# Weighted rows scattered by addition into one result per token, instead of two results weighed in the combine

## The reference, cut to what matters

```python
logits = jnp.einsum('bsd,de->bse', x, router_w) + router_b
probs = jax.nn.softmax(logits, axis=-1)
topk_p, topk_i = jax.lax.top_k(probs, 2)
topk_p = topk_p / jnp.sum(topk_p, axis=-1, keepdims=True)
combine = jnp.sum(one_hot(topk_i, 8) * topk_p[..., None], axis=-2)
moe = jnp.zeros_like(x)
for e in range(8):
    moe = moe + combine[..., e:e + 1] * (gelu((x @ w1[e] + b1[e]) * gate[e]) @ w2[e] + b2[e])
shared = (gelu((x @ sw1 + sb1) * sgate) @ sw2 + sb2) * sigmoid(shared_weight)
y = layernorm(moe + shared) * ln_g + ln_b
out = x_attn + tanh(g_ffn) * y        # x = layernorm(x_attn) above
```

## Time and profile before

| | |
|---|---|
| median of 3 runs | 1027.6 us (1027.29 to 1041.74) |
| the profiled execution | 1027.21 us, of which span 1025.4 |
| PE busy | 721.9 us (70%) |
| DVE busy | 741.0 us (72%) |
| POOL busy | 601.7 us (59%) |
| ACT busy | 554.5 us (54%) |
| attention, until about | 512 us (and its last quads until 537) |
| shared expert, until about | 606 us |
| experts' loop, until about | 918 us |
| combine, until | 1025.4 us |

### The profile page before, as it was taken

The page is one execution under the profiler, slowest core; times in us unless marked ns, Lnnn a source line. Parts: engine busy times, 40 slices in busy tenths (PEclk is TensorE's granted clock), DMA queues, the critical chain, the costliest instruction groups (busy, mean ns, idle before and its releaser), DMA issues. The chain is left out here.

```text
span 1025.4 us, 26459 instructions
## 1 busy us (share of the span) xinstructions
PE 721.9 (70%) x7850; PEld 570.9 (56%) x7851; DVE 741.0 (72%) x2078; ACT 554.5 (54%) x1131; POOL 601.7 (59%) x658
## 2 busy tenths in 40 slices
PE   2888778788777788777535899998888888850000
PEld 1556555555555555555424788888888888740000
DVE  5699999988999999889653975444444444436997
ACT  2777656677666677655212345555555554526553
POOL 5454666756666757665518904666666666650544
PEclk9899999999999999998856899999999999985555
DMA  4211222122212123000107201222222222215442
GB/s 119 50 38 47 59 54 61 35 66 62 63 50 59 34 67 84 28 15 30 42 31 228 65 3 52 62 61 60 62 62 62 59 62 57 62 53 153 127 119 82
DMA packets 91301, 66.19 MB, mean 65 GB/s; under 512 B 17009, under 2 KB 80753, under 8 KB 91249
## 3 DMA queue, kind: packets, MB, share of 16 engines
q1 hardware_dynamic: 70048, 35.49, 13.8%
q0 software_dynamic: 8448, 17.45, 5.4%
q10 hardware_dynamic: 12752, 12.58, 3.6%
HBM read 38.21 MB, written 23.09 MB: 60 GB/s over the span
## 5 line engine op out<-in xcount | busy, mean ns | idle before, releaser
L834 POOL TENSOR_TENSOR prob<-prob,mx 128x1024 f32<-128x1024 f32 x64 | 121.6, 1900 | 148.5 <-DVE mx L536 148.4
L1286 POOL DMA_INDIRECT expert_results<-y,dest x136 | 148.7, 1093 | 82.7 <-POOL dest L1282 56.2
L1100 ACT ACTIVATE hT<-bank,b1g_c,gate_c 128x256 f32<-128x256 f32 x272 | 138.1, 558 | 88.2 <-issue 38.5
L166 POOL DMA_INDIRECT expert_lists<-xn,slots x128 | 125.0, 977 | 66.9 <-issue 30.6
L1041 PE MATMUL bank<-w,hT 128*128 x1088 | 139.6, 281 | 24.1 <-ACT hT L1100 20.2
L1041 PEld LDWEIGHTS bank<-w,hT 128*128 128x128 f32 x1088 | 127.2, 191 | 39.2 <-issue 39.2
L366 PE MATMUL bank<-kbd,qg 128*64 128x256 f32 x1024 | 136.6, 407 | 4.6 <-DVE prob L529 2.0
L762 ACT ACTIVATE PT<-bank 128x512 f32<-128x512 f32 x128 | 70.1, 592 | 81.4 <-PE bank L377 80.4
L383 PE MATMUL bank<-w_att,aT 128*128 128x128 f32 x128 | 33.5, 347 | 94.0 <-issue 62.5
L529 DVE TENSOR_TENSOR prob<-bank,mask 128x512 f32<-128x512 f32 x128 | 86.0, 673 | 18.6 <-PE bank L366 14.0
L366 PEld LDWEIGHTS bank<-kbd,qg 128*64 128x64 f32 x1024 | 71.0, 145 | 45.3 <-issue 16.3
(11 more groups left out here) (182 smaller groups left out, 1743.3 us busy)
## 6 DMA issues: line engine op xcount, KB each, us to landing
rows<-expert_lists SPq DMA_DIRECT2D x70, 130.0 KB
yin<-expert_results SPq DMA_DIRECT2D x16, 512.0 KB, 5.3
x_all<-in_x SPq DMA_DIRECT2D x16, 256.0 KB
ctx_in<-in_ctx SPq DMA_DIRECT2D x16, 256.0 KB
pad_k<-in_mask_BxS_ik SPq DMA_DIRECT2D x16, 256.0 KB
xn2T<-x2T ACTq DMA_DIRECT2D x16, 256.0 KB
out<-res ACTq DMA_DIRECT2D x7, 512.0 KB, 3.2
expert_results<-y,dest POOLq DMA_INDIRECT x136
```

What stands on the lines that cost most here:

```text
L166: po.indirect_dma_start(lists[:, :], bass.IndirectOffsetOnAxis(ap=m.slots[:, par, t, k:k + 1], axis=0), m.xn2[:, par, t, :], None).then_in ...
L834: po.tensor_tensor(ps, ps, mx[:, u, :].unsqueeze(2).broadcast_to([P, H, S]), ALU.subtract).then_inc(subbed, 1)
L1100: ac.activation(hT[:, par, c, :], h_ps[par][c // 2][:, (c % 2) * SL:(c % 2 + 1) * SL], ACT.Gelu, bias=b1g_c[:, c, bass.ds(e, 1)], scale=ga ...
L1286: po.indirect_dma_start(results[:, :], bass.IndirectOffsetOnAxis(ap=dest[:, par, h, :], axis=0), y[:, par, h, :], None).then_inc(sent[par] ...
```

## The change

The weights travel with the rows. `ROW` grows from 130 to 132 values: behind first expert and token number stand w1 - w2 and w2. POOL's placing becomes share = (first expert == e) * (w1 - w2) + w2, the weight of this expert for this token, and the destination is the token number itself. DVE multiplies y by share into a new buffer `yw`, and the scatters *add* yw to one row for each token. So the table must be cleared: SP's queue stores zeros, 256 KB a quad in attention and five more at the start of the experts' program, and POOL waits for all of them ahead of the loop. As a token's two experts may stand in steps that follow each other, POOL waits before the scatters of step t until those of step t-1 have landed. In the combine one load a group takes the place of two, one add that of three operations, and ACT's weighing is gone; the 14 steps of the normalisation now all stand among the statistics, and ACT scales one group behind instead of two.

```diff
-ROW = D + 2
+ROW = D + 4
-RB_STEPS = 5
+RB_STEPS = 6
...
+            def clear(q):
+                sp.dma_start(results[bass.ds(q * QW, QW), :].rearrange("(t p) d -> p t d", p=P),
+                             m.zeros[:, :].unsqueeze(1).broadcast_to([P, QT, D])).then_inc(m.zeroed, 16)
             load(0, 0)
             load(1, 1)
+            sp.wait_ge(m.zeros_set, 1)
+            clear(0)
+            clear(1)
             if NQ // 2 > 1:
                 with sp.Fori(1, NQ // 2) as j:
                     load(j * 2, 0)
+                    clear(j * 2)
                     load(j * 2 + 1, 1)
+                    clear(j * 2 + 1)
...
                 elif i == 5:
                     need(ve, rb_step, q, per=RB_STEPS, k=2, total=NQ)
-                    ve.tensor_copy(weight[:, tiles, 0], s2)
-                    ve.tensor_tensor(weight[:, tiles, 1], p2, s2, ALU.mult)
+                    ve.tensor_tensor(w2nd, p2, s2, ALU.mult).then_inc(rb_step, 1)
...
                 elif i == 6:
                     need(ve, xn2_ready, q, per=QT, total=NQ)
+                    need(ve, rb_step, q, per=RB_STEPS, k=4, total=NQ, apart=True)
                     ve.tensor_scalar(xn2[:, par, :, D], r_m[:, 1], -1.0, float(E), ALU.mult, ALU.add)
+                    ve.tensor_tensor(xn2[:, par, :, D + 2], s2, w2nd, ALU.subtract)
+                    ve.tensor_copy(xn2[:, par, :, D + 3], w2nd)
                     ve.tensor_copy(xn2[:, par, :, D + 1], cst[:, bass.ds(q * QT + C_TOKEN, QT)])
...
+            spare = (E + 1) * SL
+            for at in range(0, spare, QW):
+                n = min(QW, spare - at)
+                sp.dma_start(results[TOK + at:TOK + at + n, :].rearrange("(t p) d -> p t d", p=P),
+                             m.zeros[:, :].unsqueeze(1).broadcast_to([P, n // P, D])).then_inc(m.zeroed, 16)
...
             def take_meta(t, par, i):
                 ve.wait_ge(rows_in[par], i * 16 + 16)
                 if not isinstance(t, int) or t >= 2:
-                    ve.wait_ge(destf_step, (t - 1) * 2)
+                    ve.wait_ge(placed, (t - 1) * PLACED)
...
                 ve.wait_ge(b2_ready, t + 1)
+                ve.wait_ge(y_done, t + 1)
+                ve.tensor_tensor(y[:, par], y_ps[par][:, 0:2 * D].rearrange("p (h d) -> p h d", d=D),
+                                 b2_now[:, par, 0:D].unsqueeze(1).broadcast_to([P, 2, D]), ALU.add).then_inc(y_taken, 1)
                 if not isinstance(i, int) or i >= 1:
                     ve.wait_ge(sent[par], i * 32)
-                ve.wait_ge(y_done, t + 1)
-                ve.tensor_tensor(y[:, par], y_ps[par][:, 0:2 * D].rearrange("p (h d) -> p h d", d=D),
-                                 b2_now[:, par, 0:D].unsqueeze(1).broadcast_to([P, 2, D]), ALU.add).then_inc(y_ready, 1)
+                wait_apart(ve, placed, t * PLACED + 3)
+                ve.wait_ge(y_taken, t + 1)
+                ve.tensor_tensor(yw[:, par], y[:, par], share[:, par].unsqueeze(2).broadcast_to([P, 2, D]),
+                                 ALU.mult).then_inc(y_ready, 1)
...
-                po.tensor_scalar(destf[:, par], meta[:, par, :, 0], b2_now[:, par, D:D + 1], -float(TOK),
-                                 ALU.is_equal, ALU.mult).then_inc(destf_step, 1)
-                po.wait_ge(destf_step, t * 2 + 1)
-                po.tensor_tensor(destf[:, par], destf[:, par], meta[:, par, :, 1], ALU.add).then_inc(destf_step, 1)
+                po.tensor_scalar(share[:, par], meta[:, par, :, 0], b2_now[:, par, D:D + 1], None,
+                                 ALU.is_equal).then_inc(placed, 1)
+                po.wait_ge(placed, t * PLACED + 1)
+                po.tensor_tensor(share[:, par], share[:, par], meta[:, par, :, 2], ALU.mult).then_inc(placed, 1)
+                po.wait_ge(placed, t * PLACED + 2)
+                po.tensor_tensor(share[:, par], share[:, par], meta[:, par, :, 3], ALU.add).then_inc(placed, 1)
                 if not isinstance(i, int) or i >= 1:
                     po.wait_ge(sent[par], i * 32)
-                wait_apart(po, destf_step, t * 2 + 2)
-                po.tensor_copy(dest[:, par, :, 0], destf[:, par]).then_inc(dest_ready, 1)
+                wait_apart(po, placed, t * PLACED + 3)
+                po.tensor_copy(dest[:, par, :, 0], meta[:, par, :, 1]).then_inc(placed, 1)
+
+            def body(t, par, i):
+                place(t, par, i)
+                if par or not isinstance(i, int) or i >= 1:
+                    wait_apart(po, sent[1 - par], i * 32 + 32 * par)
+                wait_apart(po, placed, t * PLACED + PLACED)
                 wait_apart(po, y_ready, t + 1)
                 for h in range(2):
                     po.indirect_dma_start(results[:, :], bass.IndirectOffsetOnAxis(ap=dest[:, par, h, :], axis=0),
-                                          y[:, par, h, :], None).then_inc(sent[par], 16)
+                                          yw[:, par, h, :], None, compute_op=ALU.add).then_inc(sent[par], 16)
...
+                wait_apart(ve, y_in[par], i * 16 + 16)
+                ve.tensor_tensor(acc[:, par], yin[:, par],
+                                 shared[:, bass.ds(g * GW, GW)].rearrange("p (t d) -> p t d", d=D),
+                                 ALU.add).then_inc(acc_step, 1)
...
-            BEHIND_ADD = ((0, 1), (2, 3), (4,))
-            BEHIND_STATS = ((5,), (6, 7), (8,), (9, 10), (11,), (12, 13), (), ())
+            BEHIND_STATS = ((0, 1), (2, 3), (4, 5), (6, 7), (8, 9), (10, 11), (12,), (13,))
...
             def body(g, par, i):
-                weigh(g, par, i)
-                if later(g):
-                    scale(g - 2, par)
-                if later(g) and not (isinstance(g, int) and g < 3):
-                    store(g - 3, 1 - par)
-            groups(ac, body, pairs=2)
+                scale(g, par)
+                if later(g) or g == 1:
+                    store(g - 1, 1 - par)
+            groups(ac, body)
```

More of the change, by code:

```diff
@@ L922, in experts @@
         SHARED_IN = 16 * 7
+        PLACED = 4
+        CLEARED = 16 * (NQ + 5)
         def wait_apart(eng, s, value):
@@ L1251, in _ @@
                 for h in range(2):
-                    last = po.tensor_scalar(pad_rows[:, e, h, D + 1:ROW], cst[:, C_PART:C_PART + 1],
-                                            float(2 * TOK + e * SL + h * P), None, ALU.add)
+                    last = po.tensor_scalar(pad_rows[:, e, h, D + 1:D + 2], cst[:, C_PART:C_PART + 1],
+                                            float(TOK + e * SL + h * P), None, ALU.add)
             last.then_inc(pads_ready, 1)
@@ L1303, in combine @@
         sb, sem = tools(nc, ctx)
-        yin = sb("yin", [P, 2, 2, GT, D])
+        yin = sb("yin", [P, 2, GT, D])
         acc = sb("acc", [P, 2, GT, D])
-        first = sb("first", [P, 2, GT, D])
-        second = sb("second", [P, 2, GT, D])
         normed = sb("normed", [P, 2, GT, D])
@@ L1347, in load @@
                 if later(g):
-                    sp.wait_ge(acc_step, (g - 1) * A_STEPS)
-                for k in range(2):
-                    sp.dma_start(yin[:, par, k], results[bass.ds(g * GW + k * TOK, GW), :]
-                                 .rearrange("(t p) d -> p t d", p=P)).then_inc(y_in[par], 16)
+                    sp.wait_ge(acc_step, g - 1)
+                sp.dma_start(yin[:, par], results[bass.ds(g * GW, GW), :]
+                             .rearrange("(t p) d -> p t d", p=P)).then_inc(y_in[par], 16)
             groups(sp, load)
@@ L1356, in add @@
             def add(g, par, i):
[L1358 to L1372 removed]
+                if later(g):
+                    ve.wait_ge(scaled, (g - 1) * GT)
+                wait_apart(ve, y_in[par], i * 16 + 16)
+                ve.tensor_tensor(acc[:, par], yin[:, par],
+                                 shared[:, bass.ds(g * GW, GW)].rearrange("p (t d) -> p t d", d=D),
+                                 ALU.add).then_inc(acc_step, 1)
             def stats(g, par, t):
                 if t == 0:
[L1376 removed]
+                    wait_apart(ve, acc_step, g + 1)
                 ve.bn_stats(st[:, par, t, :], acc[:, par, t, :]).then_inc(stat_step, 1)
@@ L1408, in norm @@
                 ins.then_inc(n_step, 1)
-            BEHIND_ADD = ((0, 1), (2, 3), (4,))
-            BEHIND_STATS = ((5,), (6, 7), (8,), (9, 10), (11,), (12, 13), (), ())
+            BEHIND_STATS = ((0, 1), (2, 3), (4, 5), (6, 7), (8, 9), (10, 11), (12,), (13,))
             def body(g, par, i):
-                ve.wait_ge(y_in[par], i * 32 + 32)
-                chained = later(g) or g == 1
-                for k in range(A_STEPS):
-                    add(g, par, k)
-                    if chained:
-                        for step in BEHIND_ADD[k]:
-                            norm(step, g - 1, 1 - par)
+                add(g, par, i)
                 for t in range(GT):
                     stats(g, par, t)
-                    if chained:
+                    if later(g) or g == 1:
```

(22 more changed lines are left out.)

64 lines of the change are left out of this document (24 added, 40 removed).

## The result

| | before | after |
|---|---|---|
| median of the runs timed side by side | 1027.76 us (4 runs, 1027.29 to 1041.74) | 1158.85 us (4 runs, 1156.96 to 1161.54) |
| profiled execution | 1027.21, span 1025.4 | 1156.96, span 1155.1 |
| first scatter of the loop starts | 624.20 | 625.82 |
| last scatter ends | 917.75 | 1051.77 |
| combine's first load is issued | 920.31 | 1054.67 |

A forecast was written before the change was run, and what follows sets the result against it. POOL's in-order program bounds the loop; then the landing ring does at 5.5 us a step. 1027.2 + 80 (loop) + 1 + 3 + 2 - 5.4 (combine) = 1107.8, say 1108 us; forecast case 1088 to 1156, range 1061 to 1190.

The forecast's parts named there:

- What bounds the loop: Experts' loop of before: POOL's in-order program sets the pace at 4.32 us a step; PE, at 4.0, is only just faster.
- By its program alone POOL needs 4.85 us a step: Experts' loop: 4.32 us plus 0.5 for the small tensor_tensor, waits, marks and the multiply ahead of the first scatter.
- the addition: Scatters of the experts' loop: adding in memory costs one more trip, 0.75 us on a 4.75 us ring, so 5.5 a step.
- the upper bound: Experts' loop: the addition costs at most one more landing of a small store, 2.2 us, so 6.95 us a step.
- the ring that I had built: Experts' loop: first scatter to second 1.4, second to landing 2.5, landing to first scatter 0.85: 4.75 us with plain scatters.
- Landing hidden: Rival, experts' loop: the addition costs at most 0.2 us, POOL's program stays the limit at 4.85 to 4.95, about 1064; chance 0.22.
- Long addition: Rival, experts' loop: the addition takes a whole further landing, 6.95 us a step, +179, about 1207 us; chance 0.18.
- Not slower: Rival, experts' loop: POOL's gaps take in the added work, step under 4.5 us, 1027 us; chance 0.07.
- Clock: Rival, experts' loop: PE's granted clock falls to 0.50, its step becomes 8.0 us, time at least about 1279; chance 0.03.
- The last landing: Between loop and combine: the last scatter lands later by the addition's trip, +1 us before the combine may start.
- Attention and shared expert: Before the experts' loop: small DVE instructions and routing writes cost +3 us in attention, clears +2 us in the shared expert.
- Combine: After the loop: first scaling 9.6 us earlier, but +4.2 over six groups as normalising steps follow the add; -5.4 us.

The follow-up runs named there:

- the kernel with both edits: The kernel before, its three placing operations moved from POOL to DVE and its combine unrolled with four acc buffers: median 956.15 us, 0.9414 times before.
- the run with two tables: The changed kernel with even and odd steps adding into a table each, without the wait for the landing of the step before: 1144.95 us, 6.02 a step.

## Why the prediction was right, and where its sum was off

The direction and the range held, and POOL's program and the landing were the two things to look at. But 1158.85 us lies just above the 1088 to 1156 that I called the forecast, and it is within the range only because its upper end, 6.7 us a step, makes room for most of a whole further landing. By its own sign ("wrong if ... the scatters themselves take POOL much longer than 1.1 us") the prediction had the main cost in the wrong place: they take 1.61. That the range covers it is in part luck.

**What bounds the loop: right.** POOL's in-order program sets the pace of before, not PE, the busiest engine. Lengthening a scatter by 0.52 us lengthened the step by twice that (before with adding scatters); taking the placing away shortened it. One number beside it was wrong: "PE, at 274 / 68 = 4.0 us a step, is only just faster". With the placing on DVE, PE does its step in 3.50 us, so 0.8 us lay free under POOL. The 274 us of the earlier trace rows are a busy time, and their stretch begins 18 us ahead of the loop. Between 640 and 840 us PE is busy 179.65 us in before, 0.90 of a step or 3.88 us; the same instructions at the same clock take 3.50 where PE is the limit. The single matmul is hardly shorter there (second layer 278 ns against 282), but they follow each other more closely, and what overlaps counts once. A busy time is no lower bound of a step.

**By its program alone POOL needs 4.85 us a step: right for what was counted.** With plain scatters the measured step is 4.86. So close a hit is in part luck: 4.32 + 0.5 is 4.82 and was rounded up, and one part was wrong: I had priced the multiply's place behind the placing (+0.46); the row shows a cast 0.26 longer beside the multiply and a third operation of 0.28. The earlier trace rows also shows only one of two kinds of step: there the first scatter lasts 1.08, in the steps between 1.32. What was not in this number at all is the scatter instruction's own length.

**The mis-sized term: the addition.** I kept the scatter at 1.09 us and gave all of the addition to the landing, +0.75 us, with the remark that a longer instruction would lie within the upper bound. It did, but it was the main thing:

| term, us a step | forecast | measured |
|---|---|---|
| third placing operation, marks, multiply | in 4.85 | +0.54 (4.32 to 4.86) |
| two adding scatters in POOL's program | 0 | +1.16 (4.86 to 6.02; 1.02 in before) |
| wait for the landing, beyond the program | 5.5 - 4.85 = +0.65 | +0.25 (6.02 to 6.26) |
| step | 5.5 | 6.26 |

The error is a wrong place rather than a wrong size of one event. "It should be nearest to one more trip to memory" took the addition for work of the DMA engines; the runs show most of it to be time of the engine that issues the transfer: 1.61 us on average instead of 1.09. It goes with 144 packets for 128 rows instead of 32; that the packets are what takes the time is likely, but no run varies them apart from the addition. POOL pays for each scatter, a landing is paid once a step and only beyond what POOL does meanwhile. So the ring that I had built holds with other terms: first scatter to second 1.9 (forecast 1.4), second scatter to release 732.84 - 728.54 - 0.85 = 3.45 (forecast 2.5 + 0.75 = 3.25), and 0.85: 6.2, measured 6.26. The 3.45 is what is left of after's interval if 0.85 is the reaction, and the run with the placing on DVE has it too. Of the 0.76 us that the forecast lacks, 0.5 are the first scatter's length and 0.2 the landing's, which has the second one's in it: the landing's +0.75 was made of the right amount from the wrong source, as some 0.5 of the measured +0.95 is the instruction and 0.3 to 0.4 the trip.

**The rivals.** *Landing hidden* (4.85 to 4.95 a step) is what happens with plain scatters; with adding ones it falls, though for another reason than that I gave: even without the wait POOL's program takes 6.02. *Long addition* (6.95) falls, as the landing is 0.95 us later and not 2.2, but its step is no farther from 6.26 than mine (0.69 against 0.76). *Not slower* falls: the 0.84 us gap is a reaction and not a fixed time; it was 0.82 to 0.91 behind the cast where POOL's program alone had grown (before with adding scatters, and after with plain ones), and 1.20 or 1.60 where the landing came later. *Clock*: PE was granted 0.90 in the loop on average, not 1.00 as I had expected of it, so for a part of the time the lower of its two levels. It cost nothing, since PE needs 292.55 / 424 of 6.26, 4.3 us a step, and waits for POOL.

**The last landing: right in its number, by luck in its cause.** Forecast +1 us for the trip; the load follows the last scatter's start by 4.48 instead of 3.52, +0.96. 0.62 of it is the instruction (1.58 against 0.96) and 0.34 the trip.

**Attention and shared expert: too high, and within the noise.** Forecast +5 up to the first scatter, +1.6 in the profile. As this part moves by more than that from one profile to the next, neither number is shown to be right.

**Combine: right.** Forecast -5.4, measured -4.7; first scaling 12.9 us behind the load, measured 13.1; groups 12 us apart, measured 11.8 to 12.3; the earlier trace rows has 11.3 to 11.4. The ring of scaling, held add and normalising steps took back most of what the missing load and weighing gave, as the working said; the same combine on the loop of before gives 99.2 us.

## What to carry to other kernels

Ask of a transfer that adds in memory what it costs the engine that issues it, ahead of what it costs on the way: each issue pays, and it pays in the engine's program, which no further buffer hides. Where an engine works through an order of small steps with short gaps, its busy share hides that it sets the pace; look at who starts without waiting for another engine, and then move its small operations to an engine that waits, as here three operations of 0.2 to 0.3 us, moved from POOL to DVE, were worth 40 us. And before a wait is blamed, take it away: here it was 17 of 132 us.

## What the hardware showed that I had not expected

- An indirect scatter of 128 rows of 512 bytes lasts 0.96 us on POOL where no copy of DVE falls on it and up to 1.47 where one does; with addition it lasts 1.54 to 1.60 and up to 2.0, and makes 144 packets instead of 32.
- Behind an adding scatter POOL's next operation is recorded from before the scatter's end, 0.91 us instead of 0.31 long, and ends 0.35 us behind that end as ever. Its length is a record's, and adds nothing to the step.
- DVE's copy of 128x1024 between SBUF buffers and a scatter of POOL hold each other up, so semaphores are not all that couples the engines here. A copy that still runs when the scatter starts makes it longer by what is left of the copy, less 0.12 us. In the kernel with both edits the copy ends at 640.99, 0.52 us after the scatter's start at 640.47, and the scatter lasts 1.36 instead of 0.96, 0.40 longer; in after with the placing on DVE 0.59 and 0.48 us of copy made 0.47 and 0.35 us. A copy that starts later has no single price: 0.4 to 0.5 us into an adding scatter it costs neither anything (after: scatter at 726.65 for 1.58, copy at 727.08 for 0.69); at 0.64 both are longer (scatter at 720.38 for 1.67, copy at 721.02 for 0.94); at 1.0, in the run with two tables, the scatter lasts 1.80. Into a plain one, at 0.5 us, it costs the scatter 0.37 in every other step of before (first two lines), while in before with the placing on DVE the scatter keeps its 0.96 and the copy takes 0.90 (last two lines):

```profile
710.60 1.33 POOL L1286 DMA_INDIRECT expert_results<-y,dest  x1 [0.84 <-POOL dest L1282]
711.11 0.69 DVE L1216 CAST w_now<-w 128x1024 fp32r x1 [0.55 <-issue]
...
744.33 0.96 POOL L1277 DMA_INDIRECT expert_results<-y,dest  x1 [1.54 <-DVE dest L1245]
744.89 0.90 DVE L1216 CAST w_now<-w 128x1024 fp32r x1 [0.54 <-issue]
```

- A POOL cast of 128x2 lasts 0.45 us beside DVE's multiply of two SBUF operands, and 0.18 without it.
